# Recurrent value rows on ScalarE in place of query rows, steps 10 to 15 of the first attention

## The reference

```python
def rec_step(carry, inp):
    R, h = carry
    zt, kt, vt, bt = inp
    q_rec = softmax(h)                                  # over 32 lanes of each head
    v_old = einsum('bhij,bhj->bhi', R, kt)
    R = R + (bt * (vt - v_old))[..., :, None] * kt[..., None, :]
    h = zt + einsum('bhij,bhj->bhi', R, q_rec)
    return (R, h), h
```

## Time and profile before

| | |
|---|---|
| time, median of 3 runs | 623.68 us (623.07 to 624.99) |
| time of the profiled execution | 625.58 us |
| its span (first to last instruction) | 623.8 us |
| busy, share of the span | PE 87%, DVE 69%, ACT 57%, POOL 56% |
| TensorE's clock, mean granted | 0.981 of full speed |
| the scan of the first attention | about 255 to 435 us of the span |
| steps 10 to 14 | 347.4 to 421.1 us of the span |

### The profile page before, as it was taken

How to read it: one execution, slowest core, us unless ns; L and a number is a source line. 1 busy time by engine, 2 the same in 40 slices (tenths; PEclk the granted TensorE clock), 3 DMA queues, 4 the chain that set the end, 5 groups by cost and what they waited for, 6 DMA issues and landing times.

```text
span 623.8 us, 12438 instructions
## 1 busy us (share of the span) xinstructions
PE 545.3 (87%) x4494; PEld 414.3 (66%) x4494; DVE 428.1 (69%) x1088; ACT 358.4 (57%) x949; POOL 347.1 (56%) x474
## 2 busy tenths in 40 slices
PE   7989999999987776868788888898898798989996
PEld 3556767778435565657677777785476676766785
DVE  4943663423888768799899888999424987766444
ACT  1274444444776664226688867774794668667530
POOL 2597653311350767888999899987365330001445
PEclk9999999999999989999999998999988999999999
DMA  8000000000000433200000000000000000000000
GB/s 281 13 1 1 2 0 1 1 1 2 0 2 1 78 73 72 79 0 2 2 1 1 1 2 1 2 2 0 2 2 1 1 3 1 2 2 1 9 9 18
DMA packets 10860, 10.43 MB, mean 17 GB/s; under 512 B 6000, under 2 KB 9840, under 8 KB 10544
## 3 DMA queue, kind: packets, MB, share of 16 engines
q1 hardware_dynamic: 8080, 7.54, 4.3%
q0 software_dynamic: 2144, 1.75, 1.6%
q10 hardware_dynamic: 576, 0.35, 0.2%
HBM read 5.77 MB, written 0.52 MB: 10 GB/s over the span
## 4 chain that ended last, share of the span: by engine, by line
PE 30%; DVE 17%; POOL 6%; ACT 5%; issue 3%; DVEq 0%; POOLq 0%; ACTq 0%
PE bank L1437 6%; PE bank L1722 5%; PE bank L1653 4%; DVE bank L2169 3%; PE bank L1611 3%; DVE features L2163 2%; POOL features L600 2%; PE bank L1764 2%; DVE features L2139 2%; DVE features L2491 1%; PE bank L1493 1%; DVE RK L2487 1%; POOL features L620 1%; PE bank L1719 1%; PE bank L1776 1%
## 5 line engine op out<-in xcount | busy, mean ns | idle before, releaser
L1437 PE MATMUL bank<-ident,features 128*128 128x128 f32 x604 | 76.1, 275 | 11.3 <-DVE features L2139 8.2
L1437 PEld LDWEIGHTS bank<-ident,features 128*128 128x128 f32 x604 | 66.9, 142 | 18.7 <-DVE features L2139 14.1
L905 ACT ACTIVATE G<-bank,cols 128x512 f32<-128x512 f32 x64 | 43.9, 686 | 52.9 <-PE bank L1338 52.9
L600 POOL TENSOR_TENSOR features<-UV,coefs 128x1024 f32<-128x1024 f32 (+3 forms) x36 | 59.6, 1670 | 2.6 <-DVE UV L2126 2.6
L1350 PE MATMUL bank<-weights,G 128*128 128x128 f32 x512 | 59.9, 275 | 0.0
L1338 PE MATMUL bank<-xs,weights 128*128 128x512 f32 x128 | 57.8, 594 | 0.9 <-ACT xs L896 0.9
L1350 PEld LDWEIGHTS bank<-weights,G 128*128 128x128 f32 x512 | 58.5, 192 | 0.0
L2139 DVE TENSOR_TENSOR features<-UV,bank 128x1024 f32<-128x1024 f32 (+3 forms) x68 | 55.7, 863 | 1.9 <-PE bank L1437 1.2
L400 POOL TENSOR_SCALAR rstd<-mv 128x4 f32<-128x4 f32 x8 | 1.6, 195 | 91.0 <-DVE mv L412 91.0
L995 ACT ACTIVATE xs<-UV,coefs 128x32 f32<-128x32 f32 x232 | 50.3, 308 | 0.0
L995 ACT ACTIVATE sx<-UV,coefs 128x32 f32<-128x32 f32 x200 | 43.4, 307 | 0.0
(11 more groups left out here) (362 smaller groups left out, 1351.7 us busy)
## 6 DMA issues: line engine op xcount, KB each, us to landing
weights<-in_w SPq DMA_DIRECT2D x2, 1024.0 KB, 9.8
features<-in_tok SPq DMA_DIRECT2D x1, 768.0 KB, 5.7
weights<-in_ew SPq DMA_DIRECT2D x4, 128.0 KB, 3.2
weights<-in_ew SPq DMA_DIRECT2D x2, 256.0 KB, 3.1
coefs<-G POOLq DMA_DIRECT2D x16, 25.5 KB, 4.8
rows<-in_rows SPq DMA_DIRECT2D x1, 384.0 KB, 6.5
out_h<-H SPq DMA_DIRECT2D x3, 128.0 KB, 2.0
coefs<-G SPq DMA_DIRECT2D x14, 25.5 KB, 4.7
```

The lines of the kernel that those rows point to most:

```text
L600: pool.tensor_tensor(out, u, co, ALU.mult).then_inc(s["held_p"], 1)
L905: act.activation(G[:, 4 * (w % 2) + f, :], up_bank(f)[:], ACT.Gelu, bias=col("b1", 4 * i + f)).then_inc(s["tok_gelu"], 1)
L1437: last = mm(out[:, P * k:P * k + P], x[:, P * k:P * k + P], ident[:], is_transpose=True, start=first and k == 0, stop=last_ and k == n - 1 ...
```

## The change

A new list REC says how many recurrent rows ScalarE makes: 2 in steps 10 to 15, else 0. They are rows 0 and 1. VectorE's recurrent pieces then start at row 2. In exchange FIRST goes from 2 back to 4 for steps 11 to 15, and OWN from 6 to 4 (step 12: from 5 to 3). Step 10 keeps FIRST 2 and OWN 6. GpSimd's rows stay the same ones.

ScalarE makes the two rows in a new function `recurrent_rows(t)`, 8 activations each, placed behind the last own rows of the step and ahead of `state(t)`; in step 15 they stand between the fourth and the fifth gelu. VectorE scales the coefficients of the two rows in an instruction of its own, into a small SBUF tile, ahead of the scaling of the others. TensorE adds the two rows between VectorE's last piece but one and the last piece. `half` becomes 2 from step 9 on. Two semaphores are freed by giving their counts to others (`utab_mm` to `u_mm`, `mean_mm` to `router_mm`); the waits on these count one more.

```diff
+REC = [2 if t >= 10 else 0 for t in range(T)]
-FIRST = [min(t + 1, CH if t < 10 else 2) for t in range(T)]
+FIRST = [min(t + 1, 2 if t == 10 else CH) for t in range(T)]
 def last_row_alone(n):
-    return pieces(n - 1) + [(n - 1, n)] if n > 1 else [(0, 1)]
+    k = REC[n - 1]
+    return [(k + r0, k + r1) for r0, r1 in pieces(n - 1 - k)] + [(n - 1, n)]
-OWN = [0 if t < CH else {4: 1, 5: 2, 6: 3, 7: 4, 8: 4, 9: 5, 12: 5}.get(t, 6) for t in range(T)]
+OWN = [0 if t < CH else {4: 1, 5: 2, 6: 3, 7: 4, 8: 4, 9: 5, 10: 6, 12: 3}.get(t, 4) for t in range(T)]
...
+            def recurrent_rows(t):
+                act.wait_ge(s["rec_ready"], sum(REC[:t + 1]) // 2)
+                for k in range(REC[t]):
+                    for h in range(NH):
+                        last = act.activation(own[t % 2][:, 4 + k, DH * h:DH * h + DH], UV[:, k, 1, DH * h:DH * h + DH],
+                                              ACT.Copy, scale=recS[:, k, h:h + 1])
+                    last.then_inc(s["rec_p"], 1)
...
-                    half = {9: 2, 10: 2, 11: 3}.get(t, OWN[t + 1] // 2)
+                    half = 2 if t >= 9 else OWN[t + 1] // 2
                     own_rows(t + 1, 0, half)
                 if t and t + 1 < T:
                     held_out(t + 1)
                 if t + 1 < T:
                     own_rows(t + 1, half, OWN[t + 1])
+                if REC[t]:
+                    recurrent_rows(t)
                 state(t)
...
-            expert_gelus(0, 0, 0, 6)
+            expert_gelus(0, 0, 0, 4)
+            recurrent_rows(T - 1)
+            expert_gelus(0, 0, 4, 6)
             state(T - 1)
...
+            def recurrent_reads(t):
+                for k in range(REC[t]):
+                    pe.wait_ge(s["rec_p"], sum(REC[:t]) + k + 1)
+                    turned_sum(h_bank(t), own[t % 2][:, 4 + k, :], False, False, 2)
...
-                read_out("rec", t, reads_of("rec", t))
+                part = reads_of("rec", t)
+                read_out("rec", t, part[:-1])
+                recurrent_reads(t)
+                read_out("rec", t, part[-1:])
...
-                cr = bankCR[:, 0:t + 1, :]
-                ch(dve.tensor_tensor(cr, cr, smallv[:, 5, 0:NH].unsqueeze(1).broadcast_to([P, t + 1, NH]), ALU.mult))
+                k = REC[t]
+                inv = smallv[:, 5, 0:NH].unsqueeze(1)
+                if k:
+                    dve.tensor_tensor(recS, bankCR[:, 0:k, :], inv.broadcast_to([P, k, NH]), ALU.mult)\
+                        .then_inc(s["rec_ready"], 1)
+                cr = bankCR[:, k:t + 1, :]
+                ch(dve.tensor_tensor(cr, cr, inv.broadcast_to([P, t + 1 - k, NH]), ALU.mult))
```

More of the change, by code:

```diff
@@ L238, in build @@
         own = [b.rearrange("p (r n) -> p r n", n=HB) for b in (SX[:, 0:1536], XS[:, 1024:2560])]
+        recS = smallv[:, 4, 8:8 + 2 * NH].rearrange("p (r h) -> p r h", r=2)
         bankCQ = bank[2][:, 0:2 * CH * NH].rearrange("p (k r h) -> p k r h", k=2, r=CH)
@@ L306, in build @@
             consts dve_chain pool_chain
-            ln_var ln_rstd decay_exp utab_mm tables_ready u_mm mem_ready x_mm norm_scaled norm_done
+            ln_var ln_rstd decay_exp tables_ready u_mm mem_ready x_mm norm_scaled norm_done
             xb_ready tok_norm tok_T tok_hT tok_up tok_gelu tok_down tok_add
@@ L311, in build @@
             beta_exp
-            gram_mm gram_act gram_dve coef_0 coef_1 coef_2 coef_3 coef_4 copy_0 copy_1 copy_2 copy_3 copy_4 copy_last sums_done query_scaled row_ready own_p key_p held_p held_mm upd_done
+            gram_mm gram_act gram_dve coef_0 coef_1 coef_2 coef_3 coef_4 copy_0 copy_1 copy_2 copy_3 copy_4 copy_last sums_done query_scaled row_ready own_p rec_ready rec_p key_p held_p held_mm upd_done
             read_p read_mm h_exp e_sub hs_saved
             held_saved held_T h_T query_row query_p query_mm o_mm o_add
-            y_saved y_mm b2x_ready x_norm x_twice mean_mm mean_ready router_mm r_sub r_tanh r_prob r_spread
+            y_saved y_mm b2x_ready x_norm x_twice mean_ready router_mm r_sub r_tanh r_prob r_spread
             w_ready wT_mm wT_ready bias_mm base_ready w2w_pool w2w_act x_T x_xT x_up0 x_up1 x_gelu x_down y_read
@@ L1133, in _ @@
             expert_gelus(0, 1, 2, 4)
-            act.wait_ge(s["mean_mm"], 1)
+            act.wait_ge(s["router_mm"], 1)
             act.activation(meanT[:], bank[1][0:D, P:P + T], ACT.Copy, scale=1.0 / P).then_inc(s["mean_ready"], 1)
@@ L1291, in _ @@
             pe.wait_ge(s["load_tables"], 32)
-            mm(bank[0][0:VOC, 0:DT], embT[:], wupd[:], start=True, stop=True).then_inc(s["utab_mm"], 1)
+            mm(bank[0][0:VOC, 0:DT], embT[:], wupd[:], start=True, stop=True).then_inc(s["u_mm"], 1)
             pe.wait_ge(s["tables_ready"], 1)
@@ L1619, in means @@
                 if c == NC - 1:
-                    last.then_inc(s["mean_mm"], 1)
+                    last.then_inc(s["router_mm"], 1)
             tr = nc.tensor.transpose
@@ L1974, in _ @@
             one_hot(1)
-            dve.wait_ge(s["utab_mm"], 1)
+            dve.wait_ge(s["u_mm"], 1)
             dve.wait_ge(s["load_update"], 16)
@@ L1989, in memory @@
             def memory(c):
-                dve.wait_ge(s["u_mm"], c + 1)
+                dve.wait_ge(s["u_mm"], c + 2)
                 dve.tensor_tensor_scan(memT[:, 512 * c:512 * c + 512], keep[:, 512 * c:512 * c + 512],
@@ L2412, in _ @@
             CAPACITY = float(-(-N * 5 // (4 * E)))
-            dve.wait_ge(s["router_mm"], 1)
+            dve.wait_ge(s["router_mm"], 2)
             ch(tt(rout[0:T, 3, :], bank[7][0:T, 64:64 + E], row("br0", parts=T), plus))
@@ L2416, in _ @@
             small_softmax(rout[0:T, 3, :], 0, rout[0:T, 0, :]).then_inc(s["r_prob"], 1)
-            dve.wait_ge(s["router_mm"], 2)
+            dve.wait_ge(s["router_mm"], 3)
             sc = rout[0:T, 4, :]
@@ L2442, in _ @@
                mul).then_inc(s["r_spread"], 1)
-            dve.wait_ge(s["router_mm"], 3)
+            dve.wait_ge(s["router_mm"], 4)
             dve.tensor_copy(wts[:].rearrange("p t e -> p (t e)"), bank[7][:, 128:256]).then_inc(s["w_ready"], 1)
```

## The result

| | before | after |
|---|---|---|
| time, median | 623.42 us (623.07 to 624.99, 4 runs) | 632.93 us (628.81 to 634.04, 4 runs) |
| profiled execution: time, span | 625.58, 623.8 us | 634.04, 632.3 us |
| ratio of the times | | 1.0129 (95% interval 1.0089 to 1.0169) |

The change makes the kernel 9.5 us slower. The forecast was +3.5, range 624.2 to 630.2: the sign held, the size did not.

The account below looks back on a forecast made before the run. No engine was busy throughout; a chain changing engines, through GpSimd, TensorE and VectorE, set the end. Step delays 2.2 + 0.1 + 1.05 + 0.15 = +3.5 us on 623.68 gave 627.2 us, range 624.2 to 630.2.

Parts of the forecast that it names:

- its shifts: Running delay against the kernel before, step by step: +2.2 us in step 12, +2.3 in step 13, +3.35 in step 14.
- the late rows: ScalarE's recurrent rows end last, TensorE waits for them and `state` follows 0.69 us later, in steps 10, 11 and 14.
- the four at half clock: Upper bound, 1.2 us, of the handover from ScalarE's last recurrent row to `state`: its four transposing matmuls at half clock.
- several dips at 0.04: Chance of 0.04 left for several falls of TensorE's clock, giving a time above 630.2 us.
- signs of being wrong: VectorE or TensorE still last before `state` in steps 11 and 14, GpSimd's gap missing, or the clock newly falling.
- VectorE's two query rows are hidden, the scaling costs about 0.15: Steps 10 to 15: query rows overlap the state's copy and turn; the added scaling costs 0.15 us, bounds 0 to 0.30.
- Step 10's delay is absorbed in step 11: `state` of step 10 comes 0.78 us late, hidden by ScalarE's 2.60 us of idle time ahead of step 11's `held_out`.
- GpSimd gets a gap of about 2 us ahead of its key products of step 12: Expected sign in the changed profile: GpSimd, without a gap before, stands idle about 2 us there.
- rival 2: Step 11's 2.48 us falls into ScalarE's idle time in step 12; only +1.2, 624.9 us; chance 0.15 with other hiding.
- Rival 1: Timed runs before mostly lack step 12's clock fall, so the difference is 5.8 us, time 629.5 us; chance 0.2.
- Faster, because VectorE's rows were the bound: If ScalarE's rows come in time, six steps save 0.41 us of VectorE each, 2.5 us: 621.2 us; chance 0.06.
- The rule on transposes: Skill's rule that transposes do not engage TensorE's full clock, making longer waits in the scan free; weighed, contradicted in step 11.

Follow-up runs that it names:

- second profile of the changed kernel: The changed kernel run and profiled again with no edit: 634.89 us, ratio 1.014 to the kernel before.
- the filled wait: Changed kernel with three unused matmuls on TensorE ahead of its wait for the second recurrent row: 630.29 us; with two matmuls, 631.06 us.
- the query rows alone: Changed kernel without recurrent rows on ScalarE; VectorE makes all recurrent rows and still the two added query rows: 625.45 us, ratio 1.0022.
- the run with steps 12 to 14: Changed kernel with ScalarE's recurrent rows in steps 12 to 14 only and three own rows ahead of `held_out` from step 11: 624.94 us, ratio 0.9996.
- the run with a late state: Kernel before, with unread activations on ScalarE ahead of `state` (3 in step 10, 11 each in steps 11 to 14): 631.91 us, ratio 1.0122.

## Why the prediction was wrong

Every step without a dip came out within 0.1 us of its working. The second column is the forecast length, worked out from its shifts (step 11: 14.01 - 0.78 + 2.48); the third the same step at full clock (steps 10, 13 and 14 in the second profile of the changed kernel, 11, 12 and 15 in that of the filled wait); the last is the difference of the two before it.

| step | forecast | without a dip | profiled after | dip |
|---|---|---|---|---|
| 10 | 13.95 | 14.02 | 14.02 | 0 |
| 11 | 15.71 | 15.71 | 17.01 | 1.30 |
| 12 | 16.32 | 16.25 | 16.56 | 0.31 |
| 13 | 15.37 | 15.33 | 17.00 | 1.67 |
| 14 | 15.71 | 15.77 | 17.44 | 1.67 |
| 15 | 13.75 | 13.66 | 14.81 | 1.15 |
| sum | 90.81 | 90.74 | 96.84 | 6.10 |

Against 87.31 before, the late rows are 3.43 of the 9.53 us, the 3.5 of the sum. The rest, 6.10, is TensorE at 1.2 GHz. This split is that of one execution: in the second profile the dips are 2.93 of the 6.36 us, and 1.7 more lies behind step 15. The step that failed is a silent one: the step-by-step sum kept the clock of the execution before in all steps ("the four at half clock" was allowed only inside the tail), while the same text had "TensorE waiting for the rows" in steps 10, 11 and 14. The price was there, "New dips after TensorE's longer waits for rows would cost 1.5 each", and four of the five dips cost 1.15 to 1.67; but it stood in a rival at 0.2 and several dips at 0.04, and the range ended at 630.2. The last of the prediction's own signs of being wrong came true: the clock fell in steps where it had not.

Point by point:
- *VectorE's two query rows are hidden, the scaling costs about 0.15*: right. The new scaling delays the next instruction by 0.09 us in step 11 and 0.10 in step 15, and the query rows alone cost nothing that shows.
- *Step 10's delay is absorbed in step 11*: right without a dip (15.71), wrong in the profiled execution, where TensorE at half clock, not GpSimd, paced `held_out`.
- *GpSimd gets a gap of about 2 us ahead of its key products of step 12*: 2.31 with the wait filled, 3.61 in the profile after, since step 11 lost 1.30 more.
- *Step 11's delay is taken back* (rival 2): it is not. The dip-free steps 10 to 12 are 2.20 us longer than before, the running shift of the sum.
- *Step 12's own dip before* was counted as part of the kernel, and the forecast of step 12 was TensorE's end with that dip kept. The dip is gone, and the step came out as forecast because ScalarE's end had been put only 0.19 earlier; that is luck. Rival 1 asked whether the timed runs of the kernel before lack the dip. There is one profile of that kernel, so this stays open, and with it how much of the 9.5 us it makes. The query rows alone show step 12 at 15.04 without it.
- *Faster, because VectorE's rows were the bound*: the run with steps 12 to 14 gives that rival its condition, and it still does not come true; in steps 12 and 13 GpSimd is behind VectorE. The prediction also misread one step here: it says that steps 12 and 13 just make the point, but by its own working step 13 misses it by 0.23.
- *The clock after waits.* Four of the five dips of the profile after begin behind waits of 1.13 to 1.26 us for a row and 0.47 or 0.48 for the state, and the run with a late state has dips behind waits of 1.89 and 3.07 us. The Trainium skill, "TensorE: Matmul & The Clock Gate", section "HAM oscillation — how this bites in real kernels", tells of a kernel whose clock falls at each wait for a DMA, some 3 to 5 us long, so that each next piece of work starts slow. The trace agrees in part: the pieces behind these waits start at 1.2 GHz, but the waits are for another engine, most are shorter, and a dip does not follow each time.
- *The rule on transposes.* In step 14 before, 60 transposing matmuls in a row took 6.57 us, and that step ran at 1.00; in step 13 of the second profile 56 of the 106 matmuls are transposing ones ahead of `held_out`, and the step runs at 1.00 too. The rule weighed in the prediction, that the full clock does not engage for them, is contradicted again. ("Nearly all" of the 94 matmuls of step 11 was too much: 78 are transposing ones.)

What stays open is why a given wait lowers the clock in one execution and not in the next. At the end of step 12 TensorE waits alike in three profiles of one kernel, and a dip follows in one. The dip in step 15 (1.15 us) is not explained by a longer wait: with a late state it comes behind the same 1.67 us that had none before. The times of the filled waits fell by 2.6 us only, with single runs up to 636.18, and intervals that overlap; how much the dips cost in the median is known no better than that.

## What to carry to other kernels

An engine with a low busy share can still be the last one in a step: count its instructions between the last wait ahead of the shared result and that result, and move there only what can be made without the step's own data. A forecast that makes TensorE wait longer needs the clock as a term of its sum for every lengthened wait, not as a remark at the end. Where rows must change engines, look first at where the receiving engine idles; here one row in each of four steps, moved ahead of a wait, took the ratio from 1.0129 to 1.0030.

## What the runs showed of the hardware

The same kernel gave spans of 632.3, 631.9 and 631.6 us with different dips (five in steps 10 to 15 of the first, two in each of the others, one of these twice as long), so a single profile does not fix where the clock falls. Against dip-free steps, one dip of the profile after cost between 0.31 and 1.67 us: least in step 12, where it took the place of TensorE's 1.13 us of waiting for GpSimd's held product, most in steps 13 and 14, where TensorE's queue of transposes ahead of `held_out` was on the path.
